# One-hot rows of the edge types made by GpSimd instead of VectorE, and gathers that read the index array itself

## The chip, the cores and the metric

The kernel runs on one core of a Trainium2 chip. The metric is the device time of one execution in microseconds (us). Three runs gave a median of 1069.84 us (1069.57 to 1070.19). The engines are named as in the profile: PE is TensorE's matrix multiply, PEld its load of weights, DVE is VectorE, ACT is ScalarE, POOL is GpSimd, SP is SyncE (here only a DMA queue).

## The reference

One layer of a relational graph network with 50,000 nodes, 50,000 edges, 128 features, 32 relation types and 8 basis matrices. The edges are sorted by destination.

```python
h = jnp.maximum(_layernorm(x, axis=-1), 0.0)
W_rel = jnp.einsum('rb,bdf->rdf', w_comp, weight)
seg = etype * n_nodes + dst
agg = jax.ops.segment_sum(h[src] * norm, seg, num_segments=n_rels * n_nodes)
agg = agg.reshape(n_rels, n_nodes, d_in)
node_repr = jnp.einsum('rnd,rdf->nf', agg, W_rel)
node_repr = node_repr + h_bias + h @ loop_weight
out = x + relu(node_repr)
```

For one edge this comes to: take the row x[src], normalise it, apply relu, multiply it by all 8 basis matrices, and add the 8 products with the weights norm times w_comp[type]. The result is a message, which is added at the node dst.

## The kernel before, in words

**Two phases.** The edge phase (to about 750 us) computes one message per edge and writes it to a DRAM array. The node phase (the rest) reads x and the messages of each window of 128 nodes, adds them with matrix products, and writes the output.

**The edge phase.** The edges are padded to 392 tiles of 128, taken in 98 groups of G = 4 tiles. Buffers are rings of RING = 3. For each tile, POOL issues an indirect DMA that gathers 128 rows of x into `xg`. DVE makes the statistics of tiles 0 and 1 of a group and ACT those of tiles 2 and 3. ACT subtracts the mean and applies relu (`h`), PE transposes (`hT_ps`, L728) and ACT copies back (`hT`, L638). PE then makes the 8 basis products of a tile, 128 x 1024 columns, in two halves (`products`, L706); in the records each half is two MATMUL rows, since a float32 product is made in passes. So a group has 4 x 2 x 2 = 16 rows of L706.

**Where the types come in.** For one group the kernel needs a row `hotT` of 128 x 128: partition j x 32 + r holds, for each of the 128 edges of tile j, a 1 where the type of the edge is r and otherwise a 0. It is made by one comparison of `type_bc` (the types, int32, repeated over 32 partitions by a DMA of SP, seven groups at a time) with `kind_f` (the partition's number modulo 32). PE multiplies `hotT` by `w_mix` (L722), which gives the 8 weights of each edge in `mix_ps`. DVE multiplies them by `gain` (norm over standard deviation, made by POOL) into `mix` (L1043).

**Adding the 8 products.** ACT scales products 0, 1 and 4 (`z`, L555 and L559). POOL adds products 0 and 1 (`u`, `add_pair`, L416). DVE adds products 2 and 3 onto `u` (`sum_a`) and 5, 6 and 7 onto product 4 (`sum_b`), both at L888, and adds the two (`msg`, L921). Product tiles lie in a ring of 3 in PSUM, so PE may start tile t + 3 only after the last `sum_a` of tile t.

**Order.** Every engine runs its own list of instructions in program order, with semaphores between them; nothing is reordered at run time. In step g, PE makes the products of group g - 1 and the `mix` product and transposes of group g. DVE and ACT follow the same step; POOL's loop body `gathers(g)` runs about two steps ahead with its gathers and adds pairs of group g - 3. Before the change, POOL's body begins with a copy of the group's four index columns from `src_all` into `idx` (L455), waits for that copy, and then issues the four gathers (L463) with an add behind each. DVE ends each step with `one_hot(g + 1)` (L961). Some steps hold extra work for DVE, ACT and POOL: `early_windows` prepares the first node windows (ACT L587, DVE L981 and L970, POOL's `ask_x` L440), and `row_step` makes the table of window starts on DVE.

Of the kernel before, what the change touches and what calls it, by code (L numbers as in the profile page):

```python
# [19 lines left out]
ALU = mybir.AluOpType  # L20
# [4 lines left out]
I32 = mybir.dt.int32  # L25
AX_X = mybir.AxisListType.X

P = 128
G = 4
RING = 3  # L30
TYPES = 7
# [29 lines left out]
def round_before(n, q, k=1, ring=RING):  # L61

    return n + (q - k) // ring
# [7 lines left out]
def beyond(g, n):  # L71

    return isinstance(g, int) and g >= n


def is_before(g, n):

    return isinstance(g, int) and g < n
# [12 lines left out]
def build_layer(nc, x, src, dst_cols, dst, dst_next, type_rows, norm, weight, mix_weight, loop_weight, bias, out):  # L91
    N, D = x.shape
    NT = src.shape[1]
    NG = NT // G
# [23 lines left out]
    with ctx:  # L118
        def sb(name, shape, dt=F32):
            return ctx.enter_context(nc.sbuf_tensor(name, shape, dt))  # L120
# [4 lines left out]
        def sem(name):  # L125
            return ctx.enter_context(nc.semaphore(name))
# [18 lines left out]
        src_all = sb("src_all", [P, NT], I32)  # L145
        type_bc = sb("type_bc", [P, 2, TYPES, P], I32)
        kind_i = sb("kind_i", [P, 1], I32)
        kind_f = sb("kind_f", [P, 1])
# [32 lines left out]
        xg = sb("xg", [P, RING, G, D])  # L181
# [4 lines left out]
        std = sb("std", [P, RING, G])  # L186
        h = sb("h", [P, RING, G, D])
        hT = sb("hT", [P, RING, G, P])
        idx = sb("idx", [P, RING, G], I32)
        hotT = sb("hotT", [P, RING, P])  # L190
        rstd = sb("rstd", [P, RING, G])
        gain = sb("gain", [P, RING, G])
# [42 lines left out]
        s_step = sem("s_step")  # L235
        s_src = sem("s_src")
        s_types = [sem(f"s_types{q}") for q in range(2)]
# [13 lines left out]
        s_start = sem("s_start")  # L251
        s_table = sem("s_table")

        s_idx = sem("s_idx")
        s_gather = [sem(f"s_gather{i}") for i in range(RING * G)]
        s_bn = sem("s_bn")
        s_mean = sem("s_mean")
# [2 lines left out]
        s_hot = sem("s_hot")  # L260
# [5 lines left out]
        s_mix_ps = sem("s_mix_ps")  # L266
# [140 lines left out]
        def _(pool):  # L407
# [6 lines left out]
            def add_pair(t, r):  # L414
                pool.wait_ge(s_z, t + 1)
                nc.gpsimd.tensor_tensor(u[:, r, :], z[:, r, 0, :], z[:, r, 1, :], ALU.add).then_inc(s_u, 1)  # L416

            def dst_column(g, n, q):
                if not is_before(g, RING):
                    pool.wait_ge(s_stored[q], n * 16)  # L420
                nc.gpsimd.tensor_copy(msg[:, q, :, F:C], dst_c[:, bass.ds(g * G, G)].unsqueeze(2)).then_inc(s_dst_col, 1)

            def gains(g, q):
                if is_before(g, 1):
                    pool.wait_ge(s_norm, 16)
                pool.wait_ge(s_rstd, g + 1)
                if not is_before(g, RING):
                    pool.wait_ge(s_mix, g - (RING - 1))
                nc.gpsimd.tensor_tensor(gain[:, q, :], norm_all[:, bass.ds(g * G, G)], rstd[:, q, :],
                                        ALU.mult).then_inc(s_gain, 1)  # L430
# [11 lines left out]
            def early_windows(g):  # L442

                for w in range(EARLY):
                    if g == PREP + w * PREP_STEPS - 4:
                        ask_x(w)
                    if g == PICK_STEP - 7 + w:
                        pool.wait_ge(n_seg[w], 16 * G)
                        relative(w, 0, w, n_rel)

            def gathers(g, n, q):
                if not beyond(g, NG):
                    if not is_before(g, RING):
                        pool.wait_ge(s_gather[q * G + G - 1], n * 16)
                    nc.gpsimd.tensor_copy(idx[:, q, :], src_all[:, bass.ds(g * G, G)]).then_inc(s_idx, 1)  # L455
                    pool.wait_ge(s_idx, g + 1)
                    if not is_before(g, RING):
                        pool.wait_ge(s_relu, g * G - (RING - 1) * G)
                if g == 2:
                    gains(0, 0)  # L460
                for j in range(G):
                    if not beyond(g, NG):
                        nc.gpsimd.indirect_dma_start(  # L463
                            xg[:, q, j, :], None, x, bass.IndirectOffsetOnAxis(ap=idx[:, q, j:j + 1], axis=0)
                        ).then_inc(s_gather[q * G + j], 16)
                    if j == 2 and not is_before(g, 3):
                        gains(g - 2, (q - 2) % RING)
                    if not is_before(g, 3):
                        add_pair(g * G + (j - 3 * G), (q * G + j) % RING)
                if not is_before(g, 2):  # L470
                    if is_before(g, 3):
                        pool.wait_ge(s_dst_c, 16)
                    dst_column(g - 2, round_before(n, q, 2), (q - 2) % RING)
                early_windows(g)

            sweep(pool, NG, gathers)
            gathers(NG, NG // RING, NG % RING)
            for g in range(EARLY, EARLY + 2):
                ask_x(g)
            gathers(NG + 1, (NG + 1) // RING, (NG + 1) % RING)  # L480
            for g in range(EARLY + 2, LRING):
                ask_x(g)
# [309 lines left out]
        def _(dve):  # L792
# [160 lines left out]
                if more:  # L953
                    nc.vector.bn_aggr(mv[:, aq, j, :], stats[:, aq, j, :]).then_inc(s_bn, 1)

            def one_hot(g, q):
                if not is_before(g, RING):
                    dve.wait_ge(s_mix_ps, g - (RING - 1))
                if g % TYPES == 0:
                    dve.wait_ge(s_types[g // TYPES % 2], 16 * G * (g // TYPES // 2 + 1))  # L960
                nc.vector.tensor_scalar(hotT[:, q, :], type_bc[:, g // TYPES % 2, g % TYPES, :], kind_f[:, 0:1], None,  # L961
                                        ALU.is_equal).then_inc(s_hot, 1)

            def means(g, q):
                dve.wait_ge(s_bn, g * (2 * DV) + 2 * DV)
                nc.vector.tensor_scalar(neg_mean[:, q, 0:DV], mv[:, q, :, 0], -1.0, None, ALU.mult).then_inc(s_mean, 1)
# [42 lines left out]
            def early_windows(g):  # L1009

                k, odd = (g - PREP) // 2, (g - PREP) % 2
                w, o = k // (PREP_STEPS // 2), k % (PREP_STEPS // 2)
                if not odd and 0 <= w < EARLY:
                    if o < G:
                        window_stats(w, 0, w, range(o, o + 1))
                    elif o == G:
                        window_means(w, w)
                    elif o == G + 1:
                        window_rstd(w, w)
                    else:  # L1020
                        window_shift(w, w)
                w, j = (g - PICK_STEP) // (2 * G), (g - PICK_STEP) % (2 * G) // 2
                if not odd and 0 <= w < PICKED:
                    ins = window_rows(w, w, j, j + 1)
                    if j == G - 1:
                        ins.then_inc(n_pick, 1)

            def step(g, n, q):
                more, here = not beyond(g, NG - 1), not beyond(g, NG)
                tile_slot(g, n, q, 0, more)  # L1030
                tile_slot(g, n, q, 1, more)
                if here:
                    dve.wait_ge(s_std, g + 1)
                    if not is_before(g, RING):
                        dve.wait_ge(s_gain, g - (RING - 1))
                    nc.vector.reciprocal(rstd[:, q, :], std[:, q, :]).then_inc(s_rstd, 1)
                if more:
                    means(g + 1, (q + 1) % RING)
                tile_slot(g, n, q, 2, False)
                if here:  # L1040
                    dve.wait_ge(s_gain, g + 1)
                    dve.wait_ge(s_mix_ps, g + 1)
                    nc.vector.tensor_tensor(mix[:, q, :, :],  # L1043
                                            mix_ps[:, P:P + G * B].rearrange("p (t b) -> p t b", t=G),
                                            gain[:, q, :].unsqueeze(2).to_broadcast([P, G, B]),
                                            ALU.mult).then_inc(s_mix, 1)
                tile_slot(g, n, q, 3, False)
                if more:
                    one_hot(g + 1, (q + 1) % RING)
                early_windows(g)  # L1050
                if g % ROW_EVERY == 0 and 0 < g <= ROW_STEPS * ROW_EVERY:
                    row_step(g // ROW_EVERY - 1)
# [4 lines left out]
            for j in range(DV):  # L1057
                dve.wait_ge(s_gather[j], 16)
                nc.vector.bn_stats(stats[:, 0, j, :], xg[:, 0, j, :]).then_inc(s_bn, 1)
                dve.wait_ge(s_bn, 2 * j + 1)  # L1060
                nc.vector.bn_aggr(mv[:, 0, j, :], stats[:, 0, j, :]).then_inc(s_bn, 1)
            one_hot(0, 0)
            means(0, 0)
            bin_counts(1)
            step(0, 0, 0)
            copy_hist()
            sweep(dve, NG - 1, step, first=1)


# [79 lines left out]
            g = NGW - 2  # L1149
# [4 lines left out]
            g = NGW - 1  # L1154
# [50 lines left out]
```

## Time and profile before

| What | Value |
|---|---|
| Median of three runs | 1069.84 us |
| The profiled execution's own time | 1069.31 us |
| Its span (first to last instruction) | 1067.5 us |
| PE busy | 1046.6 us (98%) |
| DVE busy | 1019.9 us (96%) |
| ACT busy | 926.3 us (87%) |
| POOL busy | 807.2 us (76%) |
| Granted TensorE clock, mean over the span | 0.999 |

A busy share is a mean over both phases and says nothing of who waits for whom. POOL's 76%, for example, holds an edge phase in which it is busy 86% and a node phase in which it is busy about half the time. A row of a timeline gives the start of an instruction, its duration, and in brackets the idle time of its engine before it with what ended it. Two instructions in a row on one engine overlap in these records, so the engine's pace is read from start to start, not from durations.

### The profile page before, as it was taken

What the parts mean: (1) busy time and instruction counts of PE and PEld (TensorE: products, weight loads), DVE (VectorE), ACT (ScalarE), POOL (GpSimd) and SP (SyncE); (2) the same over time, 40 slices, a digit from 0 to 9 for tenths busy, and PEclk for the clock granted to TensorE, in tenths of its full rate; (3) what the DMA queues carried; (4) which work ended last, traced back from release to release, by engine and by line L of the source; (5) the groups of instructions that cost most, each with busy time, mean ns of one, the idle gap of its engine ahead of it and who ended that gap; (6) DMA issues with size and microseconds to landing.
All of it is one profiled execution on the core that took longest, in us unless ns stands there. A gap on an engine that the chain in (4) does not pass through costs nothing. (4 is left out here: it accounts for less than half of the span.)

```text
span 1067.5 us, 23588 instructions
## 1 busy us (share of the span) xinstructions
PE 1046.6 (98%) x4903; PEld 661.0 (62%) x4903; DVE 1019.9 (96%) x4370; ACT 926.3 (87%) x3252; POOL 807.2 (76%) x1381
## 2 busy tenths in 40 slices
PE   4999999999999999999999999999999999999997
PEld 2444444444444444444444444444799999999997
DVE  6999999999999999999999999999999999999995
ACT  6999999999999999999999999999588888888884
POOL 7888888888888888888888888886455555555553
PEclk9999999999999999999999999999999999999999
DMA  4323232323232435232332323222599999999993
GB/s 105 95 76 88 72 100 68 93 65 103 65 95 73 124 111 137 75 85 74 83 81 77 89 72 92 76 68 79 165 298 299 297 295 297 296 300 299 296 297 99
DMA packets 91092, 150.97 MB, mean 141 GB/s; under 512 B 18578, under 2 KB 57826, under 8 KB 90946
## 3 DMA queue, kind: packets, MB, share of 16 engines
q0 software_dynamic: 28224, 76.93, 26.2%
q1 hardware_dynamic: 61250, 71.78, 21.9%
q10 hardware_dynamic: 1472, 0.74, 0.3%
q8 instruction: 40, 0.66, 0.3%
q14 instruction: 106, 0.87, 0.3%
HBM read 97.88 MB, written 51.49 MB: 140 GB/s over the span
## 5 line engine op out<-in xcount | busy, mean ns | idle before, releaser
L706 PE MATMUL y_ps<-w_all,hT 128*128 128x512 f32 x1568 | 693.8, 594 | 1.8 <-DVE sum_a L888 1.5
L706 PEld LDWEIGHTS y_ps<-w_all,hT 128*128 128x128 f32 x1568 | 286.7, 190 | 336.9 <-issue 268.2
L463 POOL DMA_INDIRECT xg<-x,idx x392 | 390.1, 995 | 76.0 <-issue 49.4
L559 ACT ACTIVATE z<-y_ps,mix 128x128 f32<-128x128 f32 x784 | 245.0, 364 | 61.1 <-PE y_ps L706 55.3
L888 DVE SCALAR_TENSOR_TENSOR sum_b<-y_ps,mix,sum_b 128x128 f32<-128x128 f32 x784 | 265.4, 339 | 0.0
L416 POOL TENSOR_TENSOR u<-z 128x128 f32<-128x128 f32 x392 | 182.0, 464 | 36.9 <-ACT z L559 31.8
L512 POOL DMA_DIRECT2D out<-res x98 | 76.1, 777 | 133.0 <-DVE res L1127 133.0
L587 ACT ACTIVATE hw<-xw,shift,nrstd 128x128 f32<-128x128 f32 x392 | 162.6, 482 | 1.7
L773 PE MATMUL y_ps<-w_loop,hwT 128*128 128x128 f32 x782 | 151.1, 274 | 0.0
L776 PE MATMUL y_ps<-seg,pick 97*128 97x128 f32 x782 | 151.1, 274 | 0.0
L774 PE MATMUL y_ps<-seg,pick 96*128 96x128 f32 x782 | 151.1, 274 | 0.0
L888 DVE SCALAR_TENSOR_TENSOR sum_b<-y_ps,mix,z 128x128 f32<-128x128 f32 x392 | 134.8, 344 | 14.6 <-ACT z L555 10.1
L555 ACT ACTIVATE z<-y_ps,mix 128x128 f32<-128x128 f32 x392 | 140.7, 359 | 3.2 <-PE y_ps L706 3.1
L888 DVE SCALAR_TENSOR_TENSOR sum_a<-y_ps,mix,u 128x128 f32<-128x128 f32 x392 | 133.7, 341 | 3.2 <-POOL u L416 3.1
L618 ACT ACTIVATE h<-xg,neg_mean 128x128 f32<-128x128 f32 x392 | 135.6, 401 | 0.1
L888 DVE SCALAR_TENSOR_TENSOR sum_a<-y_ps,mix,sum_a 128x128 f32<-128x128 f32 x392 | 133.6, 341 | 1.6 <-DVE sum_b L888 1.5
L970 DVE TENSOR_TENSOR pick<-iota_n,rel 96x1024 f32<-96x1024 f32 (+2 forms) x107 | 119.1, 1113 | 0.0
L773 PEld LDWEIGHTS y_ps<-w_loop,hwT 128*128 128x128 f32 x782 | 118.3, 191 | 0.5 <-issue 0.5
L774 PEld LDWEIGHTS y_ps<-seg,pick 96*128 96x128 f32 x782 | 118.4, 191 | 0.0
L776 PEld LDWEIGHTS y_ps<-seg,pick 97*128 97x128 f32 x782 | 118.3, 190 | 0.0
L921 DVE TENSOR_TENSOR msg<-sum_a,sum_b 128x128 f32<-128x128 f32 x392 | 116.0, 296 | 0.0
L981 DVE BATCH_NORM_STATS2 nstats<-xw 128x6 f32<-128x128 f32 x392 | 90.4, 276 | 0.0
(93 smaller groups left out, 1201.9 us busy)
## 6 DMA issues: line engine op xcount, KB each, us to landing
seg<-msgs SPq DMA_DIRECT2D x391, 96.8 KB, 3.7
msgs<-msg SPq DMA_DIRECT2D x98, 258.0 KB
xw<-x POOLq DMA_DIRECT2D x97, 256.0 KB, 5.1
out<-res POOLq DMA_DIRECT2D x97, 256.0 KB, 4.2
type_bc<-type_rows SPq DMA_DIRECT2D x56, 112.0 KB, 3.6
xg<-x,idx POOLq DMA_INDIRECT x392, 2.6
w_all<-weight ACTq DMA_DIRECT2D x1, 512.0 KB, 7.7
dst_i<-dst ACTq DMA_DIRECT2D x1, 196.0 KB, 3.2
```

The costliest lines, as they stand in the source:

```text
L416: nc.gpsimd.tensor_tensor(u[:, r, :], z[:, r, 0, :], z[:, r, 1, :], ALU.add).then_inc(s_u, 1)
L463: nc.gpsimd.indirect_dma_start(xg[:, q, j, :], None, x, bass.IndirectOffsetOnAxis(ap=idx[:, q, j:j + 1], axis=0)).then_inc(s_gather[q * G ...
L555: nc.scalar.activation(z[:, r, 2, :], y_ps[r][:, B // 2, :], ACT.Copy, scale=mix[:, q, j, B // 2:B // 2 + 1]).then_inc(s_z_high, 1)
L559: ins = nc.scalar.activation(z[:, r, b, :], y_ps[r][:, b, :], ACT.Copy, scale=mix[:, q, j, b:b + 1])
L587: return nc.scalar.activation(hw[:, r, j, :], xw[:, q, j, :], ACT.Relu, bias=shift[:, r, j:j + 1], scale=nrstd[:, r, j:j + 1])
L618: nc.scalar.activation(h[:, q, j, :], xg[:, q, j, :], ACT.Relu, bias=neg_mean[:, q, j:j + 1]).then_inc(s_relu, 1)
L706: nc.tensor.matmul(y_ps[r][:, b0:b0 + B // 2, :], hT[:, q, j, :], w_all[:, b0:b0 + B // 2, :], start=True, stop=True).then_inc(done, 1)
L773: nc.tensor.matmul(y, hwT[:, r, j, :], w_loop[:, :], start=True, stop=False)
L774: nc.tensor.matmul(y, pick[:, r, j, 0, :][0:SEG_P], seg[0:SEG_P, q, j, 0, 0:F], start=False, stop=False)
L776: mm = nc.tensor.matmul(y, pick[:, r, j, 1, :][0:SEG_P + 1], seg[0:SEG_P + 1, q, j, 1, 0:F], start=False, stop=True)
L888: return nc.vector.scalar_tensor_tensor(out=acc, in0=y_ps[r][:, base, :], scalar=c[:, base:base + 1], in1=first, op0=ALU.mult, op1=ALU.add)
L970: return nc.vector.tensor_tensor(pick[0:SEG_P, r, first:windows, :, :].rearrange("p j c n -> p (j c) n"), iota_n[0:SEG_P, :].unsqueeze(1). ...
```

## The change

POOL no longer copies index columns. The gathers take their offsets from `src_all` directly, and the tensor `idx` and its semaphore are gone. The comparison that makes `hotT` is the same instruction with the same operands, now issued by POOL: for group g - 1 behind the second gather of `gathers(g)`, for group 0 behind the four gathers of group 0. DVE's `one_hot` is gone.

```diff
-        idx = sb("idx", [P, RING, G], I32)
...
+            def one_hot(g, q):
+                if not is_before(g, RING):
+                    pool.wait_ge(s_mix_ps, g - (RING - 1))
+                if g % TYPES == 0:
+                    pool.wait_ge(s_types[g // TYPES % 2], 16 * G * (g // TYPES // 2 + 1))
+                nc.gpsimd.tensor_scalar(hotT[:, q, :], type_bc[:, g // TYPES % 2, g % TYPES, :], kind_f[:, 0:1], None,
+                                        ALU.is_equal).then_inc(s_hot, 1)
...
             def gathers(g, n, q):
                 if not beyond(g, NG):
                     if not is_before(g, RING):
-                        pool.wait_ge(s_gather[q * G + G - 1], n * 16)
-                    nc.gpsimd.tensor_copy(idx[:, q, :], src_all[:, bass.ds(g * G, G)]).then_inc(s_idx, 1)
-                    pool.wait_ge(s_idx, g + 1)
-                    if not is_before(g, RING):
                         pool.wait_ge(s_relu, g * G - (RING - 1) * G)
...
                         nc.gpsimd.indirect_dma_start(
-                            xg[:, q, j, :], None, x, bass.IndirectOffsetOnAxis(ap=idx[:, q, j:j + 1], axis=0)
+                            xg[:, q, j, :], None, x, bass.IndirectOffsetOnAxis(ap=src_all[:, g * G + j:g * G + j + 1], axis=0)
                         ).then_inc(s_gather[q * G + j], 16)
+                    if j == 1 and not is_before(g, 2) and not beyond(g, NG + 1):
+                        one_hot(g - 1, (q - 1) % RING)
...
+                if g == 0:
+                    pool.wait_ge(s_step, 2)
+                    one_hot(0, 0)
...
                 tile_slot(g, n, q, 3, False)
-                if more:
-                    one_hot(g + 1, (q + 1) % RING)
                 early_windows(g)
...
-            one_hot(0, 0)
             means(0, 0)
```

On POOL, in one round of the loop (the second round that holds all its parts), before:

```order
L455 COPY idx<-src_all 128x4
L463 DMA xg<-x,idx 128x128
L416 TENSOR_TENSOR u<-z 128x128
L463 DMA xg<-x,idx 128x128
L416 TENSOR_TENSOR u<-z 128x128
L463 DMA xg<-x,idx 128x128
L429 TENSOR_TENSOR gain<-norm_all,rstd 128x4
L416 TENSOR_TENSOR u<-z 128x128
L463 DMA xg<-x,idx 128x128
L416 TENSOR_TENSOR u<-z 128x128
L421 CAST msg<-dst_c 128x4
```

The same round on POOL after:

```order
L465 DMA xg<-x,src_all 128x128
L414 TENSOR_TENSOR u<-z 128x128
L465 DMA xg<-x,src_all 128x128
L426 TENSOR_SCALAR hotT<-type_bc,kind_f 128x128
L414 TENSOR_TENSOR u<-z 128x128
L465 DMA xg<-x,src_all 128x128
L435 TENSOR_TENSOR gain<-norm_all,rstd 128x4
L414 TENSOR_TENSOR u<-z 128x128
L465 DMA xg<-x,src_all 128x128
L414 TENSOR_TENSOR u<-z 128x128
L419 CAST msg<-dst_c 128x4
```

The copy at the head of the round is gone, and a comparison stands between the second gather and the second add.

On POOL at the start of the program, behind the iotas, before:

```order
L455 COPY idx<-src_all 128x4
L463 DMA xg<-x,idx 128x128 x4
L455 COPY idx<-src_all 128x4
L463 DMA xg<-x,idx 128x128 x4
L455 COPY idx<-src_all 128x4
L429 TENSOR_TENSOR gain<-norm_all,rstd 128x4
L463 DMA xg<-x,idx 128x128 x4
L421 CAST msg<-dst_c 128x4
L455 COPY idx<-src_all 128x4
L463 DMA xg<-x,idx 128x128
L416 TENSOR_TENSOR u<-z 128x128
```

The same place after:

```order
L465 DMA xg<-x,src_all 128x128 x4
L426 TENSOR_SCALAR hotT<-type_bc,kind_f 128x128
L465 DMA xg<-x,src_all 128x128 x4
L435 TENSOR_TENSOR gain<-norm_all,rstd 128x4
L465 DMA xg<-x,src_all 128x128 x2
L426 TENSOR_SCALAR hotT<-type_bc,kind_f 128x128
L465 DMA xg<-x,src_all 128x128 x2
L419 CAST msg<-dst_c 128x4
L465 DMA xg<-x,src_all 128x128
L414 TENSOR_TENSOR u<-z 128x128
```

Ahead of the first add there were four copies; now there are two comparisons.

On DVE at the end of a step, before:

```order
L888 SCALAR_TENSOR_TENSOR sum_b<-y_ps,mix,sum_b 128x128
L921 TENSOR_TENSOR msg<-sum_a,sum_b 128x128
L961 TENSOR_SCALAR hotT<-type_bc,kind_f 128x128
L888 SCALAR_TENSOR_TENSOR sum_b<-y_ps,mix,z 128x128
L888 SCALAR_TENSOR_TENSOR sum_a<-y_ps,mix,u 128x128
```

The same place on DVE after:

```order
L895 SCALAR_TENSOR_TENSOR sum_b<-y_ps,mix,sum_b 128x128
L928 TENSOR_TENSOR msg<-sum_a,sum_b 128x128
L895 SCALAR_TENSOR_TENSOR sum_b<-y_ps,mix,z 128x128
L895 SCALAR_TENSOR_TENSOR sum_a<-y_ps,mix,u 128x128
```

The first add of the next step now follows directly on the last message.

## Rows read from the trace of the kernel before

**Rows 1.** The page's busy line, and its rows of groups.
```profile
PE 1046.6 (98%) x4903; PEld 661.0 (62%) x4903; DVE 1019.9 (96%) x4370; ACT 926.3 (87%) x3252; POOL 807.2 (76%) x1381
...
L416 POOL TENSOR_TENSOR u<-z 128x128 f32<-128x128 f32 x392 | 182.0, 464 | 36.9 <-ACT z L559 31.8
```

**Rows 2.** Timeline of PE in the edge phase: start, duration, engine, line.
```profile
31.33 0.30 PE L722 MATMUL mix_ps<-w_mix,hotT 128*128 128x32 f32 x2
...
39.25 0.30 PE L722 MATMUL mix_ps<-w_mix,hotT 128*128 128x32 f32 x2
...
46.73 0.30 PE L722 MATMUL mix_ps<-w_mix,hotT 128*128 128x32 f32 x2
...
54.57 0.30 PE L722 MATMUL mix_ps<-w_mix,hotT 128*128 128x32 f32 x2
...
182.29 0.30 PE L722 MATMUL mix_ps<-w_mix,hotT 128*128 128x32 f32 x2
...
189.88 0.30 PE L722 MATMUL mix_ps<-w_mix,hotT 128*128 128x32 f32 x2
...
746.20 0.30 PE L722 MATMUL mix_ps<-w_mix,hotT 128*128 128x32 f32 x2
```

**Rows 3.** Waits from 100 to 750 us: us in total, times, longest.
```profile
PEld y_ps L706 <- DVE sum_a L888: 57.4, 172, 1.0
...
POOL u L416 <- ACT z L559: 26.8, 70, 1.9
```

**Rows 4.** Groups of instructions from 100 to 750 us: busy, mean ns, idle before.
```profile
L587 ACT ACTIVATE hw<-xw,shift,nrstd 128x128 f32<-128x128 f32 x16 | 7.8, 486 | 0.0
```

**Rows 5.** Timeline of POOL, parts of two rounds.
```profile
125.59 0.27 POOL L421 CAST msg<-dst_c 128x4 f32<-128x4 int32 x1
125.82 0.24 POOL L455 COPY idx<-src_all 128x4 int32<-128x4 int32 x1
126.33 0.98 POOL L463 DMA_INDIRECT xg<-x,idx  x1 [0.27 <-POOL idx L455]
...
127.95 1.06 POOL L463 DMA_INDIRECT xg<-x,idx  x1 [0.16 <-issue]
...
130.77 0.22 POOL L429 TENSOR_TENSOR gain<-norm_all,rstd 128x4 f32<-128x4 f32 x1
130.92 0.47 POOL L416 TENSOR_TENSOR u<-z 128x128 f32<-128x128 f32 x1
```

**Rows 6.** Timeline of POOL at the start of the program.
```profile
0.85 0.22 POOL L409 IOTA iota_i<- 128x128 int32 x1 [0.40 <-POOLq L1162]
...
8.88 0.94 POOL L463 DMA_INDIRECT xg<-x,idx  x1 [0.30 <-issue]
9.82 0.23 POOL L455 COPY idx<-src_all 128x4 int32<-128x4 int32 x1
10.32 0.96 POOL L463 DMA_INDIRECT xg<-x,idx  x1 [0.27 <-POOL idx L455]
...
20.83 0.18 POOL L455 COPY idx<-src_all 128x4 int32<-128x4 int32 x1
21.29 0.96 POOL L463 DMA_INDIRECT xg<-x,idx  x1 [0.27 <-POOL idx L455]
22.26 0.47 POOL L416 TENSOR_TENSOR u<-z 128x128 f32<-128x128 f32 x1
```

**Rows 7.** Timeline of DVE: one late add, and the end of a step.
```profile
22.76 0.35 DVE L888 SCALAR_TENSOR_TENSOR sum_a<-y_ps,mix,u 128x128 f32<-128x128 f32 x1 [1.76 <-POOL u L416]
...
171.00 0.28 DVE L961 TENSOR_SCALAR hotT<-type_bc,kind_f 128x128 f32<-128x128 int32 x1
171.20 0.14 DVE L872 TENSOR_TENSOR mode_f<-mode_f,hist 1x1 f32<-1x1 f32 x1
```

**Rows 8.** Timeline of PE at the start of the program.
```profile
24.04 1.12 PE L706 MATMUL y_ps<-w_all,hT 128*128 128x512 f32 x2 [1.24 <-DVE sum_a L888]
```

**Rows 9.** The messages' add from 100 to 750 us: ns min/median/max.
```profile
L921 DVE TENSOR_TENSOR msg<-sum_a,sum_b x346: 268/281/588, 101.4 to 749.6; 128x128 f32<-128x128 f32 x173
```

More of the change, by code:

```diff
@@ L252, in build_layer @@
         s_table = sem("s_table")
-        s_idx = sem("s_idx")
         s_gather = [sem(f"s_gather{i}") for i in range(RING * G)]
@@ L954, in tile_slot @@
                     nc.vector.bn_aggr(mv[:, aq, j, :], stats[:, aq, j, :]).then_inc(s_bn, 1)
[L956 to L962, printed above, removed]
             def means(g, q):
```

## The prediction

> **What bounds the kernel now.** I began with the busy line [rows 1]: PE 98%, DVE 96%. Two engines this full do not say which one waits, so I went to PE's timeline and took the `mix` product (L722), one per group, as the tick of the edge phase [rows 2]. From 39.25 to 46.73 us is one group: 7.48 us. The last tick is at 746.20 us. Between 39.25 and 746.20 lie 94 groups in 706.95 us; 94 x 7.48 is 703.12. Nearly all groups therefore run at 7.48 us, and the stalls of the whole stretch add up to 706.95 - 703.12 = 3.8 us. 7.48 us is PE's own work, since no group in the stretch is shorter while the work beside it on the other engines varies. So PE bounds the edge phase, and everything that a relief of DVE can win there is inside these 3.8 us. The list of waits shows 57.4 us of PEld waiting for `sum_a` [rows 3]; that is a wait of the weight load, which runs ahead of the products, and not a wait of PE: the ticks show that most of it costs nothing.
>
> The 3.8 us have two parts. In 16 groups ACT does one extra activation for the first node windows (L587, 16 of them, 486 ns each [rows 4]); such a group takes 189.88 - 182.29 = 7.59 us [rows 2], 0.11 more, 1.7 us in all. The other 2.1 us are stalls of over 0.05 us in nine groups (one of them also an ACT group), and some crumbs. They are the steps in which DVE has extra work or loses time to POOL; the largest but two is 54.57 - 46.73 = 7.84 us, 0.36 over [rows 2], behind a scan of the row table on DVE.
>
> The node phase has no `hotT` and no gather of edges, and PE's products fill it. The change does not touch it.
>
> **The change part by part.**
>
> *DVE loses the comparison.* It starts at 171.00 and the next instruction at 171.20 [rows 7], so 0.20 us per step, 97 times, 19 us of DVE's time. In an ordinary group this is worth nothing, because PE is the bound there; DVE will only wait longer for ACT's `z`. In the 16 ACT groups it is worth nothing either, since DVE waits for ACT in them. In the DVE groups the first 0.20 us of each stall goes, and a little more where DVE had carried a delay over from the step before. Of the 2.1 us I take 1.6. The bounds are 0 and 2.1.
>
> *POOL loses the copy.* In the round the CAST starts at 125.59 and ends at 125.86, and the next gather starts at 126.33 [rows 5]. A gather stands 0.16 us behind the end of what precedes it where no copy is in between (127.95 [rows 5]), so it would start at 126.02: the copy with its wait costs POOL 0.31 us per round. That the gathers read `src_all` should change nothing in their own duration of about 1 us: there is still one 4-byte index in each partition. No row shows it; a gain or a loss there is possible, and each 0.1 us per gather would be 0.4 us per round, so it is the same risk as that of the next part.
>
> *POOL gains the comparison.* No row shows a TENSOR_SCALAR on POOL. From below: an iota, which writes 128 x 128 and reads nothing, takes 0.22 us [rows 6]. The add of two 128 x 128 inputs takes 0.464 us [rows 1]. From above, the longest POOL instruction of the round is the gather at 0.98 us [rows 5]. The comparison reads one large input and writes one, so I take 0.40 us, between the iota and the add and nearer to the add. An instruction that follows a short one starts before its end (gain 0.22 us, next start 0.15 later [rows 5]), so the comparison holds POOL for about 0.06 less, 0.34 us.
>
> Can POOL afford it? It waits for `z` 26.8 us in 650 us [rows 3]. At 706.95 / 94 = 7.52 us a group there are 86 groups, so it has 0.31 us of slack in 7.52: it needs about 7.21 us. After: 7.21 - 0.31 + 0.34 = 7.24 us, still under 7.48. POOL becomes the bound when the comparison holds it for more than 7.48 - 6.90 = 0.58 us, that is at a duration of about 0.64 us. Below that the cover holds: the comparison stands behind the second gather and delays the second add of `u`, which had started late by as much as the copy had cost; both shifts nearly cancel (-0.31 + 0.34). The first add of a round comes 0.31 us earlier.
>
> The Trainium skill's page "GPSIMD Engine Reference", section "Performance pitfalls for Q7 kernels", gives about 2.03 cycles per element for a loop that compares, unless it is unrolled by two. At the page's 1.2 GHz that is 0.22 us for 128 elements beside the fixed part. With the small multiply's 0.22 us as that part my estimate by that page is 0.43 us, and the sum would stay where it is. The same page's section "When to use GPSIMD" advises VectorE for elementwise work; that rule speaks against the change, and it holds here only if the cover of 0.58 us is gone.
>
> *PE's tick.* `hotT` is ready earlier than before relative to its use, by the order of the lists: POOL makes row g - 1 in the round that runs beside step g - 2. No wait on it is expected behind the first group.
>
> *The start.* PE stands for 1.24 us until 24.04 us [rows 8], for a `sum_a` that waited 1.76 us for the first `u` [rows 7], which is at 22.26 behind 13 gathers [rows 6]. Each copy between gathers costs 10.32 - 9.82 = 0.50 us, of which 0.30 is the distance two gathers keep anyway (8.88 [rows 6]), so 0.20; the fourth copy costs 21.29 - 20.83 = 0.46, less the 0.16 a gather keeps and some overlap with the CAST before it, about 0.24. The first saves about 0.2 and the one ahead of the `gain` about 0.3. That is 0.9 in all. Two comparisons come in, at 0.34 plus 0.16 less the 0.30 where a gather follows: I count 0.2 and 0.3, rounded. The first comparison takes the place of a copy. Net the first `u` comes 0.3 to 0.4 us sooner, and PE with it: -0.3. The second group after it is still catching up on DVE, from 31.33 to 39.25 us by the ticks [rows 2], 0.44 over 7.48; the lighter DVE gives back some 0.2. Bounds for the start: +0.4 (comparison of 0.98 us twice) and -1.2.
>
> *Sum.* -1.6 - 0.3 - 0.2 = -2.1 us, less 0.1 for new meetings of POOL and DVE (below): -2.0. The profiled execution took 1069.31 us (span 1067.5), so 1067.3; the median of the runs is 0.53 above it. I forecast 1067.8 us for the median.
>
> **The rivals.**
>
> *POOL becomes the bound (slower).* The comparison holds POOL for more than 0.58 us, or gathers from `src_all` are longer. The place is the second add of each round: `u` comes late, DVE's `sum_a` waits, PE's tile t + 3 waits. For it: nothing in the trace shows the instruction, and POOL's waits are only 0.31 us a group. Against it: the two-input add is 0.46 us. Price: at a duration of 0.70 us the round is 6.90 + 0.64 = 7.54, 0.06 over, times 94 is 5.6 us on top of the forecast, 1073.4. At 0.98 us it is 6.90 + 0.92 = 7.82, 0.34 over and 32 us, about 1100.
>
> *DVE does not profit (no change).* DVE's add of `msg` reads two inputs from SBUF and takes 281 ns in the median and up to 588 [rows 9]. If it meets a reading POOL instruction more often now, the 0.2 us given back is lost in one such meeting (+0.2 to 0.3 us). Then only the start is left: 1069.84 - 0.3 = 1069.5. For it: those long adds. Against it: POOL's copy, which read too, is gone, and the second add keeps its place. The Trainium skill's page "SBUF — State Buffer", section "Who interferes with whom", states that a DVE instruction with two SBUF inputs contends with a GpSimd instruction that reads SBUF; the spread of `msg` agrees with it.
>
> *More comes back than I count.* POOL's first add 0.31 us earlier and DVE 0.20 lighter together may also shorten the ACT groups (1.7 us) and the start by 1.0: 1069.84 - 1.7 - 2.1 - 1.0 = 1065.0. Against it: in the ACT groups DVE waits for ACT itself.
>
> **How the numbers follow.** My forecast 0.50, POOL as the bound 0.22, no profit 0.16, more back 0.12. About 0.2% (2.1 us) is what a measurement of this kernel can tell from no change. My forecast's own range is 1066.6 to 1069.0, so it lies on that border: 0.28 of it counts as faster and 0.22 as same. Faster 0.28 + 0.12 = 0.40; same 0.22 + 0.16 = 0.38; slower 0.22. The range 1065.0 to 1074.0 leaves out most of the POOL case, about 0.18, and little below.
>
> **What would show it.** Right: L722's ticks stay at 7.48 us in ordinary groups and 7.59 in the ACT groups, and the group behind the tick at 46.73 stalls less than 0.36; the comparison on POOL is 0.35 to 0.50 us; POOL still waits for `z`; the first `u` starts before 22.0 us. Wrong: a comparison over 0.64 us, gathers over 1.1 us, DVE's `sum_a` waiting for `u` in every group, or ticks evenly above 7.48.

## The result and the profile after

The changed kernel takes 1092.01 us (median of 4 runs, 1091.78 to 1092.35) against 1070.01 us of the kernel before on the same chip: ratio 1.0201, 95% interval 1.0189 to 1.0213, slower by 22.0 us. The forecast was 1067.8 us, with a range up to 1074.0.

The page of the changed kernel. The span is 1090.6 us, 23.1 more than before. POOL has gained 55 us of busy time. Its idle time ahead of the adds, 36.9 us in [rows 1] (31.8 of them for `z`), is down to 13.5 us (9.0 for `z`).

```profile
PE 1065.1 (98%) x4903; PEld 648.1 (59%) x4903; DVE 1037.0 (95%) x4272; ACT 932.4 (86%) x3252; POOL 862.3 (79%) x1381
...
L414 POOL TENSOR_TENSOR u<-z 128x128 f32<-128x128 f32 x392 | 189.5, 483 | 13.5 <-ACT z L566 9.0
```

The ticks of the edge phase, from PE's timeline, as in [rows 2].

```profile
40.30 0.30 PE L729 MATMUL mix_ps<-w_mix,hotT 128*128 128x32 f32 x2
...
560.72 0.30 PE L729 MATMUL mix_ps<-w_mix,hotT 128*128 128x32 f32 x2
...
568.20 0.30 PE L729 MATMUL mix_ps<-w_mix,hotT 128*128 128x32 f32 x2
...
576.25 0.30 PE L729 MATMUL mix_ps<-w_mix,hotT 128*128 128x32 f32 x2
...
769.24 0.30 PE L729 MATMUL mix_ps<-w_mix,hotT 128*128 128x32 f32 x2
```

The 94 groups now take 769.24 - 40.30 = 728.94 us, 22.0 more than the 706.95 of before: the stalls have grown from 3.8 to 25.8 us. The stretch before them is 1.05 us longer, and behind it 1090.6 - 769.24 = 321.4 us are left against 1067.5 - 746.20 = 321.3: the node phase is untouched. Some groups still take 7.48 us (568.20 - 560.72), others 8.05 (576.25 - 568.20). By kind of group, from the ticks: the 16 ACT groups as before; the eight groups with a `row_step` +5.1 us, the twelve with an early pick (L969) +5.1, all others +11.8.

The waits from 100 to 750 us, as in [rows 3]. No row of POOL waiting for `z` is left here (26.8 us before), and the weight loads wait 91.7 us for `sum_a` instead of 57.4. DVE's own wait for `u` is a row of three times only.

```profile
PEld y_ps L713 <- DVE sum_a L895: 91.7, 151, 1.1
...
DVE sum_a L895 <- POOL u L414: 2.3, 3, 0.8
```

POOL's timeline in one round, as in [rows 5].

```profile
405.19 0.96 POOL L465 DMA_INDIRECT xg<-x,src_all  x1 [0.16 <-issue]
406.18 0.64 POOL L426 TENSOR_SCALAR hotT<-type_bc,kind_f 128x128 f32<-128x128 int32 x1
406.77 0.48 POOL L414 TENSOR_TENSOR u<-z 128x128 f32<-128x128 f32 x1
407.41 1.04 POOL L465 DMA_INDIRECT xg<-x,src_all  x1 [0.16 <-issue]
408.47 0.35 POOL L435 TENSOR_TENSOR gain<-norm_all,rstd 128x4 f32<-128x4 f32 x1
408.78 0.44 POOL L414 TENSOR_TENSOR u<-z 128x128 f32<-128x128 f32 x1
409.38 0.97 POOL L465 DMA_INDIRECT xg<-x,src_all  x1 [0.16 <-issue]
410.38 0.51 POOL L414 TENSOR_TENSOR u<-z 128x128 f32<-128x128 f32 x1
410.84 0.18 POOL L419 CAST msg<-dst_c 128x4 f32<-128x4 int32 x1
411.18 1.00 POOL L465 DMA_INDIRECT xg<-x,src_all  x1 [0.15 <-issue]
412.19 0.47 POOL L414 TENSOR_TENSOR u<-z 128x128 f32<-128x128 f32 x1
412.82 0.97 POOL L465 DMA_INDIRECT xg<-x,src_all  x1 [0.16 <-issue]
```

From the second gather to that of the next round it is 412.82 - 405.19 = 7.63 us, and no wait is in it: POOL is now the bound, over PE's 7.48. The comparison takes 0.64 us and holds POOL 406.77 - 406.18 = 0.59. The gain takes 0.35 us where it took 0.22 [rows 5], and holds POOL 0.31 instead of 0.15. DVE's timeline shows why: `msg` starts at the same time, and `mix` behind it waits for the gain.

```profile
408.49 0.28 DVE L928 TENSOR_TENSOR msg<-sum_a,sum_b 128x128 f32<-128x128 f32 x1
408.86 0.19 DVE L1042 TENSOR_TENSOR mix<-mix_ps,gain 128x32 f32<-128x32 f32 x1
```

This repeats in nearly every round. From 100 to 740 us the gain runs beside the message's add in 81 of 82 rounds, where before it did so in 1 of 86. The gain's 350 ns is a mean of 82 with 210 before; DVE stands 7.2 us ahead of `mix`, where it stood 0.0 before; and the early pick takes 673 ns where it took 414 (groups of instructions, 100 to 740 us):

```profile
L426 POOL TENSOR_SCALAR hotT<-type_bc,kind_f 128x128 f32<-128x128 int32 x83 | 52.3, 631 | 3.1
L435 POOL TENSOR_TENSOR gain<-norm_all,rstd 128x4 f32<-128x4 f32 x82 | 28.7, 350 | 1.6
...
L1042 DVE TENSOR_TENSOR mix<-mix_ps,gain 128x32 f32<-128x32 f32 x82 | 15.7, 191 | 7.2
...
L969 DVE TENSOR_TENSOR pick<-iota_n,rel 96x256 f32<-96x256 f32 x12 | 8.1, 673 | 0.0
```

The row of `mix` in the kernel before:

```profile
L1043 DVE TENSOR_TENSOR mix<-mix_ps,gain 128x32 f32<-128x32 f32 x85 | 15.5, 183 | 0.0
```

### The profile page after: what moved, and what is told of

Its sections match the earlier page's. It is cut to its first block and busy times, and to the rows that moved or that the text cites. A ratio compares the mean times of both kernels' runs of the same rounds, so it can differ in the third digit from the quotient of the medians.

```text
span 1090.6 us, 23396 instructions
## 1 busy us (share of the span) xinstructions
PE 1065.1 (98%) x4903; PEld 648.1 (59%) x4903; DVE 1037.0 (95%) x4272; ACT 932.4 (86%) x3252; POOL 862.3 (79%) x1381
## 5 line engine op out<-in xcount | busy, mean ns | idle before, releaser
L713 PE MATMUL y_ps<-w_all,hT 128*128 128x512 f32 x1568 | 711.4, 600 | 6.7 <-DVE sum_a L895 2.7
L713 PEld LDWEIGHTS y_ps<-w_all,hT 128*128 128x128 f32 x1568 | 273.6, 189 | 373.2 <-issue 264.5
L465 POOL DMA_INDIRECT xg<-x,src_all x392 | 387.9, 990 | 66.7 <-issue 61.5
L414 POOL TENSOR_TENSOR u<-z 128x128 f32<-128x128 f32 x392 | 189.5, 483 | 13.5 <-ACT z L566 9.0
L895 DVE SCALAR_TENSOR_TENSOR sum_b<-y_ps,mix,z 128x128 f32<-128x128 f32 x392 | 130.9, 334 | 6.9 <-ACT z L562 4.7
L928 DVE TENSOR_TENSOR msg<-sum_a,sum_b 128x128 f32<-128x128 f32 x392 | 125.1, 319 | 0.0
L969 DVE TENSOR_TENSOR pick<-iota_n,rel 96x1024 f32<-96x1024 f32 (+2 forms) x107 | 122.1, 1141 | 0.0
```

The source lines that it names most:

```text
L465: nc.gpsimd.indirect_dma_start(xg[:, q, j, :], None, x, bass.IndirectOffsetOnAxis(ap=src_all[:, g * G + j:g * G + j + 1], axis=0)).then_in ...
L713: nc.tensor.matmul(y_ps[r][:, b0:b0 + B // 2, :], hT[:, q, j, :], w_all[:, b0:b0 + B // 2, :], start=True, stop=True).then_inc(done, 1)
L895: return nc.vector.scalar_tensor_tensor(out=acc, in0=y_ps[r][:, base, :], scalar=c[:, base:base + 1], in1=first, op0=ALU.mult, op1=ALU.add)
L928: nc.vector.tensor_tensor(msg[:, q, j, 0:F], sum_a[:, r, :], sum_b[:, r, :], ALU.add).then_inc(s_msg, 1)
```

## The experiments

In all of them the pitch of a POOL instruction is the time from its start to the next one's, as a median over the ordinary rounds, those with no extra instruction on POOL; "the round" is the sum of these medians. A difference in us is one to the kernel before on the same chip. A meeting is a stretch in which a POOL and a DVE instruction run at once and one or both take longer than they do alone. The expectations use these names: theory or rival A, the sum of POOL's own times is the price; B and D, its meetings with DVE are; C, the gathers from the large array are.

A sum of medians leaves out what happens in fewer than half of the rounds. In the changed kernel the mean of the ordinary round is 7.72 us, where the medians give 7.63. Most of the rest lies in two rows: the first add (a mean of 0.67, a median of 0.63) and the cast (0.40 and 0.34). From 40 to 768 us 22 of 94 casts run over 80 ns longer than 0.18 us, twelve of them beside an early pick. 94 x (7.63 - 7.48) is 14 us, and 94 x (7.72 - 7.48) is 23: the medians explain two thirds of the 22 us, the means all of it.

**Only the direct gathers.** The comparison stays on DVE.

```diff
-                        pool.wait_ge(s_gather[q * G + G - 1], n * 16)
-                    nc.gpsimd.tensor_copy(idx[:, q, :], src_all[:, bass.ds(g * G, G)]).then_inc(s_idx, 1)
-                    pool.wait_ge(s_idx, g + 1)
-                            xg[:, q, j, :], None, x, bass.IndirectOffsetOnAxis(ap=idx[:, q, j:j + 1], axis=0)
+                            xg[:, q, j, :], None, x, bass.IndirectOffsetOnAxis(ap=src_all[:, g * G + j:g * G + j + 1], axis=0)
```

> Half of the change alone: the gathers read the index array, POOL's copy and its wait are gone, the comparison stays on VectorE. Theory A (the changed kernel is slow because POOL's round, without a wait, adds up to 7.63 us and more against PE's 7.48): POOL's round falls to about 6.9 us here, PE stays the bound, the ordinary group stays at 7.48 us, and the time is 1068 to 1070 us. Rival C (offsets read from the large array make the gathers or their start slower): gathers over 1.05 us or landings later than 2.6 us, time over 1075.

Measured: 1069.86 us, ratio 0.9986 (0.9977 to 0.9995). The waits from 100 to 740 us:

```profile
POOL u L414 <- ACT z L553: 51.0, 83, 1.3
```

POOL waits 51.0 us in 83 rounds, and its round without waits is 6.81 us. The stalls of the 94 groups are 3.0 us instead of 3.8. So this half is harmless, rival C is out, and what the change costs comes with the comparison.

**Only the comparison on POOL.** The copy stays.

```diff
+                    nc.gpsimd.tensor_copy(idx[:, q, :], src_all[:, bass.ds(g * G, G)]).then_inc(s_idx, 1)
+                    pool.wait_ge(s_idx, g + 1)
```

> The other half alone: the comparison on POOL, and the copy of the index columns kept. Theory A: POOL's round is 0.40 us longer than in the changed kernel (copy to gather 0.515, the cast before it 0.12 shorter), so 94 groups x 0.40 = 38 us: about 1130 us. Rival B (it is the comparison's meetings with VectorE at the SBUF port that cost, not POOL's sum): the copy adds little, 1092 to 1100 us.

Measured: 1114.42 us, +43.1, ratio 1.040 (1.0384 to 1.0416). Both numbers of the expectations were missed. The copy and the cast hold POOL 0.447 + 0.133 us here and the cast alone 0.338 in the changed kernel, so the copy's pitch is 0.24 and not 0.40; 94 x 0.24 is 23 us, and 21 were measured. Once POOL is the bound, the kernel is longer by nearly all that POOL is given more. That is theory A for the copy; it does not say what the comparison's own 22 us are made of.

**Four columns, and 64 columns.** Both are the changed kernel with a narrower comparison; from group 3 on the other columns keep old values, so these two kernels don't compute the layer.

```diff
-                nc.gpsimd.tensor_scalar(hotT[:, q, :], type_bc[:, g // TYPES % 2, g % TYPES, :], kind_f[:, 0:1], None,
+                cols = P if is_before(g, RING) else 4
+                nc.gpsimd.tensor_scalar(hotT[:, q, 0:cols], type_bc[:, g // TYPES % 2, g % TYPES, 0:cols], kind_f[:, 0:1], None,
```

> The changed kernel, whose comparison covers only 4 of 128 columns from group 3 on (the other columns of the one-hot row keep old values). Theory A: the comparison holds POOL for about 0.15 instead of 0.59 us, the round falls to about 7.1 us, PE is the bound again with groups of 7.48, and what is left is the pure gain of a lighter VectorE: 1066.5 to 1068.5 us. If the value of that relief was overestimated: 1069 to 1070. Rival B: the short comparison meets VectorE hardly, so the same; this run does not part A from B.

> The changed kernel, whose comparison covers only 64 of 128 columns from group 3 on (the rest keeps old values). Theory A: it holds POOL for about 0.37 us, the round is about 7.25 to 7.4 us, just under PE's 7.48, and the time is 1067 to 1070 us, though a half of the reading is still there. Rival B (meetings with VectorE set the price, in proportion to the comparison's length): half of the loss stays, about 1080 us, in groups over 7.48 in which POOL still waits.

Measured: four columns 1071.55 us, +0.3, ratio 1.000 (0.9991 to 1.0009); 64 columns 1079.69 us, +8.4, ratio 1.0076 (1.006 to 1.0091). The comparison of each (groups of instructions, 100 to 740 us):

```profile
L427 POOL TENSOR_SCALAR hotT<-type_bc,kind_f 128x4 f32<-128x4 int32 x86 | 28.3, 329 | 3.2
```

```profile
L427 POOL TENSOR_SCALAR hotT<-type_bc,kind_f 128x64 f32<-128x64 int32 x84 | 39.3, 468 | 3.1
L436 POOL TENSOR_TENSOR gain<-norm_all,rstd 128x4 f32<-128x4 f32 x84 | 25.9, 309 | 1.6
```

The pitches are 0.278, 0.430 and 0.593 us for 4, 64 and 128 columns: a fixed part of 0.27 us and 2.5 ns a column. With 64 columns theory A in its plain form fails: 6.81 + 0.43 is 7.24 us, and the loss should be nil, but the round is 7.45 (7.58 as a mean), and the loss is 8.4 us. The gain's 309 ns is a mean of two kinds of round: in 56 of 84 it meets the message's add and takes some 0.35 us, in the other 28 it takes 0.22. With four columns it meets it in 7 of 85, the mean is 227 ns and the loss is gone. No gain shows from the lighter DVE; but POOL still carries 0.28 us more here, so this run alone doesn't price that relief.

**The load without the dependence.** To the kernel with direct gathers an extra instruction is added in the place of the comparison. DVE keeps its own.

```diff
+                    if j == 1 and not is_before(g, 3) and not beyond(g, NG):
+                        nc.gpsimd.tensor_scalar(spare[:, :], iota_i[:, :], kind_f[:, 0:1], None, ALU.is_equal)
```

and, in the second run,

```diff
+                        nc.gpsimd.iota(spare[:, :], [[1, 610]], base=0, channel_multiplier=0)
```

> VectorE keeps its comparison, the gathers read the index array, and POOL makes in the same place of its round a comparison of the same size on a constant array into a scratch tile: POOL's load of the changed kernel without the relief of VectorE. Theory D (POOL's own pitches, 6.81 + 0.59 = 7.40 us, would still fit into 7.48; it is the meetings of POOL's and VectorE's reads at the SBUF port, some 0.3 us a round, that push POOL over PE): as slow as the changed kernel or slower, 1090 to 1100 us, with a gain of 0.35 instead of 0.21 us. If the dependence of TensorE on a row made by POOL were the cause: near 1070.

> As the run before, but the extra POOL instruction is an iota of 610 columns, about 0.63 us like the comparison, which writes and reads nothing from SBUF. Theory D: there is nothing to meet VectorE's reads, the round adds up to 7.37 to 7.42 us and PE stays the bound: 1069 to 1073 us. Rival A (POOL's time alone, whatever it does): as slow as its neighbour with the comparison, over 1085.

Measured: with the comparison 1089.88 us, +19.1, ratio 1.0179 (1.0162 to 1.0196); with the iota 1076.99 us, +6.2, ratio 1.006 (1.0043 to 1.0077). The groups of the first and the second (100 to 740 us):

```profile
L462 POOL TENSOR_SCALAR spare<-iota_i,kind_f 128x128 f32<-128x128 int32 x83 | 52.1, 628 | 3.1
...
L958 DVE TENSOR_SCALAR hotT<-type_bc,kind_f 128x128 f32<-128x128 int32 x83 | 37.9, 456 | 0.0
...
L428 POOL TENSOR_TENSOR gain<-norm_all,rstd 128x4 f32<-128x4 f32 x83 | 27.1, 327 | 2.2
```

```profile
L462 POOL IOTA spare<- 128x610 int32 x85 | 55.8, 656 | 1.1
...
L958 DVE TENSOR_SCALAR hotT<-type_bc,kind_f 128x128 f32<-128x128 int32 x84 | 37.3, 444 | 0.0
...
L428 POOL TENSOR_TENSOR gain<-norm_all,rstd 128x4 f32<-128x4 f32 x84 | 17.6, 209 | 1.6
```

That PE depends on a row made by POOL is not what costs: 19 us come without it. The iota holds POOL even longer than the comparison (0.607 against 0.591 us), and costs a third. The rounds are 7.63 us with the comparison and 7.48 with the iota. Two rows are shorter with the iota, by 0.23 us together: the gain (pitch 0.150 against 0.304), and the gather two instructions behind (0.986 against 1.062). One is longer: the third add (0.686 against 0.601), which meets the message's add in the gain's place.

So what POOL's time alone costs is not told by these runs; 6 us is more than theory D allowed, and it has meetings in it. One of them neither the kernel before nor the changed kernel has. DVE's own comparison runs beside POOL's fourth add in 74 of 83 rounds of the first and 70 of 84 of the second, and takes 456 and 444 ns in the mean against 284 in the kernel with direct gathers. How many of the 19 and 6 us are due to it was not measured. The iota reads nothing, but it also puts POOL in another phase to DVE; these two runs don't part the one from the other.

**The gain earlier.** The changed kernel, with the gain behind the second add.

```diff
-                    if j == 2 and not is_before(g, 3):
-                        gains(g - 2, (q - 2) % RING)
                     if not is_before(g, 3):
                         add_pair(g * G + (j - 3 * G), (q * G + j) % RING)
+                    if j == 1 and not is_before(g, 3):
+                        gains(g - 2, (q - 2) % RING)
```

> The changed kernel with POOL's gain moved from before the third add to behind the second. In the changed kernel gain starts together with VectorE's msg add, takes 0.35 instead of 0.21 us and holds POOL 0.31 instead of 0.15, and VectorE's mix waits for it. Theory D: away from that meeting 0.16 to 0.2 us a round come back, 15 to 19 of the 22 us: 1073 to 1080 us. Rival A: POOL's list is as long as before, 1090 to 1093.

Measured: 1083.15 us, +12.3, ratio 1.0116 (1.0099 to 1.0132). The gain is short:

```profile
L435 POOL TENSOR_TENSOR gain<-norm_all,rstd 128x4 f32<-128x4 f32 x84 | 16.2, 193 | 0.0
```

The same instructions in another order give back 10 of the 22 us. The round is 7.49 us. It is less than expected (15 to 19 us): the second add and the gain together hold POOL for 0.79 us instead of 0.94, which is 0.14 us a round where 0.16 to 0.20 were expected, and the first add and the cast stay long in the mean (0.66 and 0.39 us).

**The comparison at the end of the round.**

```diff
                         add_pair(g * G + (j - 3 * G), (q * G + j) % RING)
+                    if j == 3 and not is_before(g, 2) and not beyond(g, NG + 1):
+                        one_hot(g - 1, (q - 1) % RING)
```

> The changed kernel with the comparison behind the fourth add instead of behind the second gather. Rival A (sum alone): 1090 to 1093 as before. Theory D: another phase between POOL and VectorE, so another time; if the row operations and picks that VectorE has at the end of its step now meet the comparison fully, it is slower, 1095 to 1105; if the gain no longer meets the msg add, 1075 to 1085.

Measured: 1079.24 us, +8.4, ratio 1.0079 (1.0062 to 1.0096). The comparison now meets the message's add itself, and both are long; the gain is not:

```profile
L928 DVE TENSOR_TENSOR msg<-sum_a,sum_b 128x128 f32<-128x128 f32 x337 | 117.2, 348 | 0.0
L426 POOL TENSOR_SCALAR hotT<-type_bc,kind_f 128x128 f32<-128x128 int32 x84 | 61.3, 729 | 0.0
L435 POOL TENSOR_TENSOR gain<-norm_all,rstd 128x4 f32<-128x4 f32 x84 | 18.0, 215 | 1.5
```

The time is inside the range given for a gain that meets the message's add no more (1075 to 1085). Rival A, the sum alone, is out: by the differences place is worth 14 of the 22 us. No place that was tried wins against the kernel before.

**What the relief of DVE is worth.** Direct gathers with the comparison on DVE over four columns (the others keep old values, so it doesn't compute the layer), and once more the direct gathers alone.

```diff
-                nc.vector.tensor_scalar(hotT[:, q, :], type_bc[:, g // TYPES % 2, g % TYPES, :], kind_f[:, 0:1], None,
+                cols = P if is_before(g, RING) else 4
+                nc.vector.tensor_scalar(hotT[:, q, 0:cols], type_bc[:, g // TYPES % 2, g % TYPES, 0:cols], kind_f[:, 0:1], None,
```

> What the relief of VectorE is worth by itself: the kernel with direct gathers and the comparison on VectorE, but over 4 of 128 columns from group 3 on (the other columns keep old values), so that VectorE gains some 0.13 us a step and POOL is untouched. If the prediction's term was right (1.6 us for 0.20 us a step), it is about 1 us faster than the kernel with direct gathers, 1068 to 1069 us. If the relief is worth nothing because TensorE and ScalarE set the pace: the same, 1069 to 1070.5 us.

> The kernel with direct gathers and the comparison on VectorE once more, beside the run before on the same chip: 0.05 to 0.25% faster than the kernel before, as in its first run (0.14%). If that was chance: a ratio of 0.9995 to 1.0005.

Measured: 1069.07 us, ratio 0.9988 (0.9979 to 0.9997), and 1069.46 us, ratio 0.9995 (0.9986 to 1.0004). The instruction on DVE fell from 284 to 228 ns, less than I had expected. By the ticks the stalls of the 94 groups are 2.75 us with the light comparison, 2.95 and 3.0 in the two runs with the full one, 3.8 before. So the relief gave some 0.2 us, from one trace of each run. The direct gathers give 0.8 to 0.9 us within the 94 groups both times; over the whole kernel the first run is faster by 0.14%, the second not clear of no change. Of the versions that compute the layer this half alone is the fastest measured, by 1.0 to 1.4 us.

## Why the prediction was wrong, point by point

*What bounds the kernel.* Right. PE's tick of 7.48 us held in every run in which POOL had room, with 2.8 to 4.8 us of stalls where 3.8 stood before.

*The comparison's size.* Sized too small: 0.631 us and a pitch of 0.593, where 0.40 and 0.34 were taken. The value was taken between two rows of other instructions, an iota that reads nothing and an add of two inputs, and the add was no upper bound. The four-column run shows what they hide, a fixed part of 0.27 us, where a gain of 128 x 4 holds POOL for 0.15. The Trainium skill, "GPSIMD Engine Reference", section "Performance pitfalls for Q7 kernels", has 2.03 cycles an element for a loop that compares. The 2.5 ns a column measured here are 3.0 cycles at the page's clock, so the estimate of 0.43 us worked out from it was too low, and the measurement decides. That page's advice of VectorE for elementwise work ("When to use GPSIMD") is borne out here: each place tried on POOL was 8 to 22 us slower with all 128 columns.

*The cover of POOL.* This is the step that failed. The sum 7.21 - 0.31 + 0.34 took all other pitches of POOL as they were and said that the comparison fits up to a duration of 0.64 us. With the measured pitch that sum is 6.90 + 0.59 = 7.49 us, about 1 us in all, and 22 were measured. So the comparison's size alone does not explain the loss; what failed is that all other pitches stay as they were. Against the direct gathers (6.81 us) the round is 7.63: 0.59 is the comparison, 0.16 the gain, and 0.07 the gather ahead of the gain; the fourth add's 0.06 more are given back by the cast (0.34 us instead of 0.43). So 0.23 us came in that no instruction was added for, and another 0.10 in the mean, in the rounds with a long first add or cast.

The two moves show that much of it hangs on order and not on load: 10 us for the gain, 14 us for the comparison. Without these 0.23 us the round would be 7.40 us, inside PE's 7.48; the first 0.08 of them make POOL the bound. From then on DVE waits for the gain ahead of `mix` in the rounds (7.2 us in 82, none before), and `msg`, which stands just ahead of `mix`, starts with the gain in 81 of them. I call the meeting shown, since the gain is 193 to 215 ns in both runs that avoid it and 350 in the one that does not. That DVE's waiting is what fixes the phase is read from the traces and was not tested; with 64 columns two rounds of three had the meeting although the plain sum leaves 0.24 us of room.

*The rival that came true* was POOL as the bound, with its sign right and its place in part: from 100 to 740 us DVE stood 5.3 us ahead of the `sum_a` that reads `u` (0.7 before), but 7.2 us ahead of `mix`, for the gain, which the rival did not name. It was given a chance of 0.22 and a decision point of 0.64 us, which the measured 0.631 does not reach; the 0.593 for which it holds POOL passes the 0.58 by 0.01. The second rival, meetings of POOL with DVE's `msg`, was priced as a loss of DVE's 0.2 us at most; it was priced on the wrong engine, for POOL had the smaller margin, and the two rivals add up.

*DVE's relief.* Not seen. It was to give 1.6 us of the 2.1. With POOL burdened by only four columns, nothing is left of it (+0.3), and the light comparison on DVE gives 0.2 us for 0.06 of duration. In proportion, an estimate, the whole 0.20 us would be worth 0.7; no run took the comparison off DVE without giving POOL something. Of the 2.1 us that I had put down to DVE, 0.8 belonged to POOL: they went with the copy alone.

*The copy.* Near enough: 0.31 us predicted, 0.40 by the difference of the rounds (7.21 to 6.81), 0.24 in the run that keeps it. *The gathers* from the large array: unchanged, 0.99 us a piece.

*The start.* Wrong in sign: the tick at 39.25 is at 40.30. The first `u`, forecast before 22.0 us, starts later than before:

```profile
18.13 0.63 POOL L426 TENSOR_SCALAR hotT<-type_bc,kind_f 128x128 f32<-128x128 int32 x1
18.92 1.02 POOL L465 DMA_INDIRECT xg<-x,src_all  x1 [0.17 <-issue]
...
22.57 0.47 POOL L414 TENSOR_TENSOR u<-z 128x128 f32<-128x128 f32 x1
```

That is 22.57 against 22.26 [rows 6]. Counted from the first gather it is 18.33 us against 17.42 before and 17.07 and 17.59 in the two runs of the direct gathers, so the two comparisons cost some 0.7 to 1.3 us there. Those two runs of one kernel have the tick at 40.68 and 39.03, so over 1.5 us of the start are chance, and a term of 0.3 us could not be told there.

*PE's wait for `hotT`* is nil, as said.

## What to carry to other kernels

Ask of each engine how long its round is without waits, not how busy it is: POOL was busy for 86% of the edge phase and had 0.3 us to give. When work moves to an engine with so little room, measure the instruction alone first, and count as load also what it shifts: here the neighbour waited for the new bound once a round, and a meeting that had happened in 1 of 86 rounds happened in 81 of 82. Two edits in one change should be timed apart; here the small one was the better half.

## What the runs showed of the hardware

A long two-input instruction on DVE can hold POOL for its whole length. In the run with four columns the scan over 400 columns took 1.24 us on DVE (0.97 before), and the cast of 128 x 4 on POOL, 0.27 us in the median of that run, took 0.88. The changed kernel has the same pair, again with a cast of 0.88. DVE first, then POOL:

```profile
52.44 1.24 DVE L869 TENSOR_TENSOR_SCAN upto<-ones_row,hist 1x400 f32<-1x400 f32 x1
```

```profile
52.31 0.52 POOL L414 TENSOR_TENSOR u<-z 128x128 f32<-128x128 f32 x1
52.78 0.88 POOL L419 CAST msg<-dst_c 128x4 f32<-128x4 int32 x1
53.81 0.98 POOL L466 DMA_INDIRECT xg<-x,src_all  x1 [0.16 <-issue]
```

The scan began while the add was running and ended at 53.68; the cast ended at 53.66. The Trainium skill, "SBUF — State Buffer", section "Who interferes with whom", states that a DVE instruction with two SBUF inputs contends with a GpSimd instruction that reads SBUF; these rows agree, and that one of them stands for the other's whole length is what they show as well.

A DVE instruction with one large input took longer as well: DVE's comparison took 0.48 us in the median where POOL's fourth add ran beside it, in both runs with an extra POOL instruction, and 0.28 with the direct gathers alone.

A narrower comparison on POOL saves little: 4 columns still cost 47% of the pitch of 128. And the gather two instructions behind a comparison on POOL takes 1.03 to 1.04 us in the median, with 128, 64 or 4 columns, where the same gather takes 0.96 in the kernel with direct gathers and in the one with the iota (0.99 in the kernel before). With the comparison at the end of the round it is the first gather that is long, 1.03 instead of 0.98. So it follows the comparison's place and hardly its width; the cause of that was not found.
